# Input laid out tile by tile and chunk by chunk in memory, with the first loads spread anew over two DMA queues, in a mixture-of-experts kernel

## What is computed

```python
g = jnp.einsum('bsd,edf->ebsf', h, Wg)          # e = 8, d = 128, f = 512
u = jnp.einsum('bsd,edf->ebsf', h, Wu)
expert_outs = jnp.einsum('ebsf,efd->ebsd', jax.nn.silu(g) * u, Wd)
expert_output = jnp.einsum('be,ebsd->bsd', gating_probs, expert_outs)
shared = jnp.einsum('bsf,fd->bsd', jax.nn.silu(h @ Sg) * (h @ Su), Sd)
...
x = x + (1.0 - sg) * expert_output + sg * shared
x = x + jnp.einsum('bij,bjk->bik', T[itok_B_1_98 - 1], x)
```

## Time and profile before

| | us |
|---|---|
| median of 3 runs | 311.44 |
| lowest and highest | 311.27, 313.25 |
| the profiled execution, whole | 311.43 |
| its span, first to last instruction | 309.6 |
| PE busy in the span | 303.3 (98%) |
| DVE, ACT, POOL busy | 214.0, 163.5, 102.5 |

### The profile page before, as it was taken

How to read it: one execution, slowest core, us unless ns; L and a number is a source line. 1 busy time by engine, 2 the same in 40 slices (tenths; PEclk the granted TensorE clock), 3 DMA queues, 4 the chain that set the end, 5 groups by cost and what they waited for, 6 DMA issues and landing times.

```text
span 309.6 us, 4555 instructions
## 1 busy us (share of the span) xinstructions
PE 303.3 (98%) x1356; PEld 251.1 (81%) x1356; DVE 214.0 (69%) x348; ACT 163.5 (53%) x303; POOL 102.5 (33%) x116
## 2 busy tenths in 40 slices
PE   5999999999999999999999999999999999999995
PEld 4788888888888888888888888888888888888884
DVE  2667766777667666677766776667766676667785
ACT  2765555555555555555555555555555555554552
POOL 2675213441145115511551144312441155180000
PEclk9999999999999999999999999999999999999999
DMA  7600300020003000110003000012000000000011
GB/s 216 233 2 0 103 1 2 0 102 1 0 0 95 6 0 0 28 74 0 0 0 111 25 25 25 25 37 90 0 0 0 0 0 0 0 2 0 34 36 68
DMA packets 5847, 10.39 MB, mean 34 GB/s; under 512 B 592, under 2 KB 4048, under 8 KB 5840
## 3 DMA queue, kind: packets, MB, share of 16 engines
q1 hardware_dynamic: 5552, 10.04, 9.7%
q10 hardware_dynamic: 288, 0.26, 0.3%
HBM read 9.25 MB, written 1.05 MB: 33 GB/s over the span
## 4 chain that ended last, share of the span: by engine, by line
PE 97%; DMA 2%; DVE 0%; ACT 0%; ACTq 0%; issue 0%
PE o_bank L404 11%; PE o_bank L405 11%; PE o_bank L407 11%; PE g_bank L378 10%; PE u_bank L378 10%; PE g_bank L379 10%; PE u_bank L379 10%; PE g_bank L380 10%; PE u_bank L380 10%; DMA w_raw<-in_W_all 2%; PE o_bank L425 1%; PE o_bank L417 0%; DVE res L324 0%; PE u_bank L417 0%; PE g_bank L438 0%; PE g_bank L441 0%
## 5 line engine op out<-in xcount | busy, mean ns | idle before, releaser
L295 DVE TENSOR_TENSOR u_bank<-u_bank,silu_g 128x512 f32<-128x512 f32 x144 | 100.8, 700 | 85.9 <-PE u_bank L380 84.2
L236 ACT ACTIVATE silu_g<-g_bank 128x512 f32<-128x512 f32 x144 | 86.1, 598 | 133.8 <-PE g_bank L380 132.3
L301 DVE TENSOR_TENSOR h_lo<-u_bank,h_hi 128x512 fp32r<-128x512 f32 x144 | 98.0, 681 | 0.1
L218 POOL TENSOR_TENSOR acc<-acc,scaled 128x512 f32<-128x512 f32 x32 | 41.4, 1295 | 163.2 <-DVE scaled L309 163.0
L242 ACT ACTIVATE h_hi<-u_bank 128x512 fp32r<-128x512 f32 x144 | 85.5, 594 | 0.7 <-DVE u_bank L295 0.7
L404 PE MATMUL o_bank<-h_hi,w_hi 128*128 128x512 f32 x144 | 56.2, 391 | 0.0
L407 PE MATMUL o_bank<-h_lo,w_hi 128*128 128x512 f32 x144 | 56.1, 389 | 0.0
L405 PE MATMUL o_bank<-h_hi,w_lo 128*128 128x512 f32 x144 | 56.0, 389 | 0.0
L378 PE MATMUL g_bank<-x_hi,w_hi 128*128 128x512 f32 x142 | 55.6, 392 | 0.0
L380 PE MATMUL g_bank<-x_hi,w_lo 128*128 128x512 f32 x142 | 55.3, 389 | 0.0
L378 PE MATMUL u_bank<-x_hi,w_hi 128*128 128x512 f32 x142 | 55.3, 389 | 0.0
(11 more groups left out here) (51 smaller groups left out, 145.2 us busy)
## 6 DMA issues: line engine op xcount, KB each, us to landing
w_raw<-in_W_all SPq DMA_DIRECT2D x8, 768.0 KB, 4.4
T_plus<-in_TT SPq DMA_DIRECT2D x16, 64.0 KB, 1.7
out_y<-res SPq DMA_DIRECT2D x3, 256.0 KB, 2.5
acc<-in_xT SPq DMA_DIRECT2D x2, 256.0 KB, 5.0
w_raw<-in_W_all SPq DMA_DIRECT2D x2, 256.0 KB, 5.4
acc<-in_xT SPq DMA_DIRECT2D x1, 512.0 KB, 6.0
w_raw<-in_W_all ACTq DMA_DIRECT2D x2, 128.0 KB, 4.9
out_y<-res SPq DMA_DIRECT2D x2, 128.0 KB, 2.4
```

The costliest lines, as they stand in the source:

```text
L218: nc.gpsimd.tensor_tensor(acc[:, t, :], acc[:, t, :], scaled[:, t % 2, :], ALU.add).then_inc(acc_done, 1)
L236: nc.scalar.activation(silu_g[:, k % 2, :], g_bank[k % 2][:, :], ACT.Silu).then_inc(g_read, 1)
L295: nc.vector.tensor_tensor(u_bank[k % HR][:, :], u_bank[k % HR][:, :], silu_g[:, k % 2, :], ALU.mult).then_inc(h_done, 1)
L301: nc.vector.tensor_tensor(h_lo[:, k % HR, :], u_bank[k % HR][:, :], h_hi[:, k % HR, :].bitcast(F32), ALU.subtract).then_inc(split_done, 1)
```

## The change

Only the layout in memory and the queue of one load are changed. `xT` becomes [tile, partition, 512], so that one tile is 256 KB in one piece. `W_all` becomes [expert, chunk, partition, matrix, 128], so that one chunk is 192 KB in one piece and a partition's row of a chunk 1536 bytes. Chunk 1's load goes from ACT's queue to SP's, behind x tile 0 and ahead of chunks 2 and 3. What lands in SBUF is the same, as are the instructions of all engines but for the DMA issues.

```diff
-                sp.dma_start(w_raw[:, slot, :, :, :], W_all[e, :, :, :, :].rearrange("a p c m f -> (a p) c m f")).then_inc(w_in[slot], 16)
+                sp.dma_start(w_raw[:, slot, :, :, :], W_all[e, :, :, :, :].rearrange("a c p m f -> p (a c) m f")).then_inc(w_in[slot], 16)
 
             def load_x(t0, t1, s):
-                sp.dma_start(acc[:, t0:t1, :], xT[:, t0:t1, :]).then_inc(s, 16)
+                sp.dma_start(acc[:, t0:t1, :], xT[t0:t1, :, :].rearrange("t p w -> p t w")).then_inc(s, 16)
 
             load_x(0, 1, x_in[0])
-            sp.dma_start(w_raw[:, 0, 2:NC, 0:2, :], W_all[0, :, 2:NC, 0:2, :]).then_inc(wc0_in[2], 16)
-            sp.dma_start(w_raw[:, 0, :, 2, :], W_all[0, :, :, 2, :]).then_inc(wd0_in, 16)
+            sp.dma_start(w_raw[:, 0, 1, 0:2, :], W_all[0, 1, :, 0:2, :]).then_inc(wc0_in[1], 16)
+            sp.dma_start(w_raw[:, 0, 2:NC, 0:2, :], W_all[0, 2:NC, :, 0:2, :].rearrange("c p m f -> p c m f")).then_inc(wc0_in[2], 16)
+            sp.dma_start(w_raw[:, 0, :, 2, :], W_all[0, :, :, 2, :].rearrange("c p f -> p c f")).then_inc(wd0_in, 16)
             load_x(1, 2, x_in[1])
...
-            for c in range(2):
-                act.dma_start(w_raw[:, 0, c, 0:2, :], W_all[0, :, c, 0:2, :]).then_inc(wc0_in[c], 16)
+            act.dma_start(w_raw[:, 0, 0, 0:2, :], W_all[0, 0, :, 0:2, :]).then_inc(wc0_in[0], 16)
             act.wait_ge(zero_done, 1)
```

More of the change, by code:

```diff
@@ L24, in moe_then_step_kernel @@
     E = W_all.shape[0] - 1
-    NC = W_all.shape[2]
+    NC = W_all.shape[1]
     K = TT.shape[0]
@@ L505, in pack @@
         e = gate.shape[0]
-        g = gate.reshape(e, P_, NC_, P_)
-        u = up.reshape(e, P_, NC_, P_)
-        d = down.reshape(e, NC_, P_, P_).transpose(0, 2, 1, 3)
+        g = gate.reshape(e, P_, NC_, P_).transpose(0, 2, 1, 3)
+        u = up.reshape(e, P_, NC_, P_).transpose(0, 2, 1, 3)
+        d = down.reshape(e, NC_, P_, P_)
         return _np.stack([g, u, d], axis=3)
@@ L514 @@
     laid = {
-        "xT": x.transpose(2, 0, 1).reshape(D_, 4, -1),
+        "xT": x.transpose(2, 0, 1).reshape(D_, 4, -1).transpose(1, 0, 2),
         "side": _np.tile(side[None, :], (P_, 1)),
```

## The result

The changed kernel takes 310.58 us in the median of 18 runs, the kernel before 312.66 us in 18 runs beside it. The ratio is 0.9938, with a 95% interval of 0.9924 to 0.9953: 1.9 us less. One run of the changed kernel, at 517.1 us with a mean granted clock of 0.56, stands alone and is not in the ratio; the other 17 lie from 309.68 to 311.76 us, those of before from 311.27 to 313.93. The forecast was 310.4 us, within 309.5 to 311.6.

A forecast was written before the change was run, and what follows sets the result against it. The prediction took the start of TensorE's unbroken stream, held up by chunk 1's load, to bound the kernel. From 311.43 it took 0.42 for chunk 1's order and 0.6 for the layout: 310.4 us, range 309.5 to 311.6.

The forecast's parts named there:

- The stream begins earlier and all of it counts: Kernel's end moves one for one with the moment at which TensorE's unbroken stream of matmuls begins.
- First term: At the start, chunk 1 loaded ahead of chunks 2 and 3 lets the first low product issue 0.42 us earlier.
- back-to-back roundings: Sign of being right: ACT's two roundings of 0.42 us, chunks 0 and 1, stand without idle time between.
- four L438 without a gap: Sign of being right: TensorE issues the first four high products without waiting for chunk 1.
- Second term: In the first load burst, the new layout lands x tile 0 and chunk 0 earlier by 0.6 us, ends 0 and 1.21.
- the other reading: By the skill's row-pitch rule, pitches of 8 KB and 2 KB are far below its figures: layout term 0, sum 311.0.
- the sign that the first L441 follows 1.6 us after chunk 0's landing: Sign of being right: TensorE's first low product is issued at chunk 0's landing plus 1.63 us.
- What is late next: After the earlier start, chunks 2 and 3 and POOL's rests before L404 could cost 0.1 us in the fastest case.
- Later loads hidden: Later experts' loads may slow with 1536-byte rows, but over 9 us to spare hides it: cost 0.
- The rival of a slow stretch that goes entirely: First loads run at 371 GB/s from 2.0 on, 1.21 us earlier: 309.8 us, or 309.5; chance 0.16.

The follow-up runs named there:

- order alone: The kernel before, old layout, with chunk 1's load moved behind x tile 0 on SyncE's queue; 312.4 us, ratio 0.998 (0.9965 to 0.9996).

## Why the prediction was right, and where its steps were not

The time lies in the range and 0.2 us from the forecast, but the gain was about twice the 1.04 us that was forecast, and the steps hold in part. That the time came out so near is partly luck: two errors nearly cancel in it, as the fifth point shows.

- *The stream begins earlier and all of it counts.* Right: the span less the start of L404 is constant within 0.3 us, as the last table shows.
- *First term, 0.42 us for chunk 1's place.* The signs came true: back-to-back roundings, four L438 without a gap. But the 0.42 us were read from a profile at full clock. In the profiles at 1.2 GHz with chunk 1 behind chunk 0, the wait for chunk 1 costs 0.01 to 0.17 us, and at full clock with the early landing POOL's rests set L404 with either order (9.38 and 9.31). Still, the times give order alone 0.6 us (interval 0.1 to 1.1), and with six warm-up matmuls the kernels with the early landing and without the order gain 0.5 to 0.8 us less than the changed one (ratios 0.9957, 0.9953 and 0.9955 against 0.9938 and 0.9932, with intervals that overlap, from different groups). With eight the medians differ by 0.1. What the order is worth with six, and by which way, stays open.
- *Second term, 0.6 us for the layout.* This is the term that was mis-sized. It measured 1.20 us (5.14 to 3.94 for x tile 0), nearly the end of 1.21 that the sum had kept for the range. The row on which 0.6 was built, a later expert's load at 156 GB/s, begins slowly too, for a reason that stays open. The cause was left open between one piece in memory and fewer places touched; it is neither, but the distance of 8192 bytes. The Trainium skill's rule on row pitches (DMA: Bandwidth & Descriptors, Latency and other measured facts), by which I had put this term at 0 as the other reading, has figures for copies with pitches from 512 KiB on. The measurement decides: here 8 KB cost 1.2 us of landing and 8448 bytes did not.
- *The weights' layout* was counted in the second term without being told apart from x's. Alone it gives 0 (ratio 1.0, 0.9986 to 1.0013).
- *TensorE's clock.* This was the step that was missing. From the column at 1.00 the prediction took it that the products run at 2.4 GHz whenever they begin. In ten of the fourteen profiled executions they begin at 1.2 GHz, and by L404 the changed kernel loses 1.4 and 1.8 us to that with six warm-up matmuls and 2.3 with none. For the same reason the sign that the first L441 follows 1.6 us after chunk 0's landing came out at 2.43 (6.56 - 4.13), against 1.75 with eight matmuls at full clock. The baseline was misread too: the profiled execution of before was one of the few with full clock at 5.9, and only 6 of the 71 runs of before that were made in all lie under 311.6 us. So the forecast of 310.4 stood on a base 1.2 us under the kernel's usual time (312.66 against 311.43), and its gain was 0.9 too small (1.9 against 1.04), or 1.0 too small by the difference of the two medians (2.1). The two errors nearly cancel in the time. Of the missing gain the landing is 0.6; the rest is not taken apart. A part of it may be that fewer products run at the low clock, nine in the changed kernel's profile against twelve in that of the weights' layout alone, but those are single executions.
- *What is late next.* Named rightly (chunks 2 and 3, then POOL's rests before L404), sized at 0.1 and measured at 0.34, at full clock.
- *Later loads hidden.* Right: 4.6 instead of 4.4 us, and no wait.

The rival of a slow stretch that goes entirely, 309.8 us, is where the lowest four runs lie (309.68, 309.83, 309.86 and 309.98), but none of them has a trace. The one profiled execution of the changed kernel's program at full clock, with eight warm-up matmuls, took 310.16 us, between the rival and the forecast.

## What to carry to other kernels

Look at the distance in memory between the pieces that the partitions read in a first load. A distance of 8192 bytes halved the rate here, and 256 bytes of padding were as good as a new layout. Keep TensorE busy up to the first real product, by more warm-up matmuls: with twelve warm-up matmuls instead of six the old kernel gained 1.6 us, more than the half of what any kernel here gained over it, and the best one has both (310.4 us, ratio 0.9911). It is no sure cure: with eight, three of four profiles still had products at 1.2 GHz up to 6.4 us or later. And judge the start of a kernel by many runs, since two single profiles of equal span hid a gain of 1.9 us.

## What the runs showed of the hardware

- TensorE's products of 512 columns begin 0.43 us apart (1.2 GHz) and go to 0.23 (2.4 GHz) at a moment that differs between executions of the same kernel: for the changed one at 4.7 at the latest and at 7.2 with eight warm-up matmuls, at 8.7 and 9.8 with six, at 10.8 with none. The profile's column of the granted clock shows 1.00 on both levels.
- The first loads, from 1.5 to 4.0 us, went at 121 to 136 GB/s with x's pieces 8192 bytes apart (172 with chunk 1 on the other queue), and at 236 to 277 GB/s with them 2048 or 8448 bytes apart.
- Loads of 768 KB took 4.5 to 4.6 us in the median in pieces of 1536 bytes (seven profiles) and 4.3 to 4.5 us in pieces of 6144 bytes (seven profiles), so the size of the piece made little or no difference.
